# A memory loop in feature-major form with a Gram-matrix correction, in a four-block network on one core

## Chip, cores and metric

One core of one Trainium2 chip. The metric is the device time in microseconds of one execution. The time of a kernel is the median over its runs.

## What is computed

A batch of 4 images, 16 x 16 positions, 64 channels, all float32, goes through four blocks, each added to its input: a test-time memory (below), a mixture of eight experts of which two are used, a stack of convolutions, and an LSTM over the 256 positions. Only the first block is touched. With its names:

```python
mem0 = ((w1_0, w2_0), (w1_1, w2_1))            # 64x128 and 128x64, twice
def _mlp(params, h):
    for w1, w2 in params:
        h = h + gelu(h @ w1) @ w2
    return h
def step(carry, x_t):                          # x_t: 4 images, 16 tokens, 64 channels
    params, mom = carry
    k = _l2norm(x_t @ Wk); v = x_t @ Wv
    lr, forget, eta = ...                      # one number per image, a mean of sigmoids
    g = grad of mean((_mlp(params, k) - v)**2)
    new_mom = eta * mom - lr * g
    new_params = params * (1 - forget) + new_mom
(paramsT, momT), _ = scan(step, (params0, mom0), swapaxes(x, 0, 1))   # 16 steps
final = mean of paramsT over the images
return _mlp(final, q)
```

Each image has its own weights. The sixteen steps depend on each other: the weights after one step are those of the next.

## The kernel before

The kernel is written with an instruction list for each engine and explicit semaphores; nothing reorders them. Stages in order: the inputs' layer norm, projections, gates (lines 322 to 354 on TensorE); the memory loop; the final pass of all 1024 tokens through the averaged weights (466 to 490); the experts; the convolutions; the LSTM (654 to 675), an unrolled loop of 256 steps in which TensorE does six small products with 64x64 weights (L651) and three or four fills (L675).

**Weights.** P holds the weights, M the momentum, each 128 partitions x 4 images x 256 columns. Columns 0:128 hold w1_0 on partitions 0:64 and w1_1 on partitions 64:128; columns 128:192 hold w2_0 and 192:256 w2_1, both over 128 partitions. Me and Pf are M and P times their gate, Q is their sum. GpSimd computes these three each step (L282, L283, L286), on whole tiles of 1024 elements a partition. The layout is the same for the four images.

**The loop.** `Fori(0, T, MEM_UN)` on every engine, four steps in the body, so four passes. GpSimd copies the step's keys, values and gates into small tiles (kcur, vcur, gcur, lrcur) one step ahead. A step works token-major in the hidden layers: tokens of image b lie on partitions 32b to 32b+15. Forward: a0 (L366, TensorE), gelu on ScalarE (L727), a transpose back to feature-major (L373) and a copy, h1 (L380), a1 (L393), gelu (L742), again a transpose and a copy, the prediction (L407). VectorE adds keys and values (L930, L933, L943) and computes the gelu's derivative from a square and a tanh of ScalarE (L927, L928, L935, L937 for the first layer, L939 to L949 for the second). Backward: L416, L438, L449 with transposes of the weights made in the same step (L375, L386, L402), and of the errors; then sixteen gradient products (L428, L456, L461, L462) into four PSUM banks, one for each image. When all are there (semaphore grads), VectorE adds them in three instructions: both halves of P (L960, L961) and M (L962). The next step's a0 waits for the first of them.

**Fills.** `keep_busy(place, bank)` (L316) issues matmuls of zeros, 256 bf16 columns each, whose result nobody reads, ahead of a wait of TensorE. BUSY gives their number at twelve places of a step: 38 in all, ten at the start, four behind a0. `busy` (L312) does the same with 512 columns outside the loop; eight such stand behind the loop and begin when P's second half is done.

**After the loop.** VectorE adds the four images' weights (L966, L967), scales them (L968), and L471 is the first product of the final pass.

Of the kernel before, what the change touches and what calls it, by code (L numbers as in the profile page):

```python
# [20 lines left out]
DE = 128  # L21
# [4 lines left out]
S = W * W  # L26
# [11 lines left out]
BUSY = (10, 4, 4, 2, 2, 0, 5, 5, 4, 0, 4, 2)  # L38
MEM_UN = 4
TP = T + MEM_UN  # L40


def wide(ap, n):

    return bass.AP(ap.tensor, ap.offset, [*ap.ap, [0, n]])
# [7 lines left out]
def build(nc, i_, out):  # L53
    with ExitStack() as ctx:
# [18 lines left out]
        memw = sb("memw", [128, 2 * DE])  # L73
# [43 lines left out]
        kk = sb("kk", [128, B, TP * C])  # L117
        qq = sb("qq", [128, NTOK])
        vT = sb("vT", [128, B, TP * C])
        kcur = [sb(f"kcur{n}", [128, B, 32]) for n in range(2)]  # L120
        vcur = [sb(f"vcur{n}", [128, B, C]) for n in range(2)]
        gcur = [sb(f"gcur{n}", [128, 3, B]) for n in range(2)]
        lrcur = [sb(f"lrcur{n}", [128, 1]) for n in range(2)]
# [12 lines left out]
        w21T = sb("w21T", [128, B, DE])  # L136
        w20T = sb("w20T", [128, B, DE])
        w11T = sb("w11T", [128, B, D])
        g0T = sb("g0T", [128, B, C])
        g1T = sb("g1T", [128, B, C])  # L140
        h1T = sb("h1T", [128, B, 32])
        dT = sb("dT", [128, B, 32])
        dh1T = sb("dh1T", [128, B, 32])
        da1T = sb("da1T", [128, B, C])
        hv = sb("hv", [128, B, C])
        a0q, a0u, a0y, a0t, a0x, a0s = (sb(f"a0{c}", [128, DE]) for c in "quytxs")
        a1q, a1u, a1y, a1t, a1x, a1s = (sb(f"a1{c}", [128, DE]) for c in "quytxs")
        g0tok = sb("g0tok", [128, DE])
        h1tok = sb("h1tok", [128, D])
        g1tok = sb("g1tok", [128, DE])  # L150
        dtok = sb("dtok", [128, D])
# [3 lines left out]
        ktok = sb("ktok", [128, D])  # L155
        FW2 = sb("FW2", [128, 2, 2 * DE])
        FW = sb("FW", [128, 2 * DE])
# [22 lines left out]
        hT = sb("hT", [128, E, HC, NTOK // 2])  # L180
        yT = [sb(f"yT{n}", [128, NTOK // 2]) for n in range(2)]
        fold = sb("fold", [128, D])
# [39 lines left out]
        def _(sp):  # L222
            sp.dma_start(xs[:, :, :], i_["x"]).then_inc(sem("ld_x"), 16)
            for dst, key, s in ((ident[:, :], "ident", "ld_id"), (wqkv[:, :], "wqkv", "ld_a"), (wgate[:, :], "wgate", "ld_a"),
                                (gaff[:, :], "gaff", "ld_g"), (gsel[:, :, :], "gsel", "ld_g"), (memw[:, :], "memw", "ld_m"),
# [15 lines left out]
        def _(pool):  # L241
            nc.gpsimd.memset(idle[:, :], 0.0)
            nc.gpsimd.memset(xnT[:, :], 0.0).then_inc(sem("idle"), 1)  # L243
            for t in (*kcur, h1T, dT, dh1T):
                nc.gpsimd.memset(t[:, :, :], 0.0)
            nc.gpsimd.memset(M[:, :, :], 0.0)
# [21 lines left out]
            def kview(tile, t, lo=0):  # L268
                return tile[lo:128, :, bass.ds(t * C, C)]
# [918 lines left out]
```

## Time and profile before

| | us |
|---|---|
| runs | 800.73, 807.91, 808.19 |
| median | 807.91 |
| the profiled execution's own time | 796.82 |
| its span, first to last instruction | 795.0 |
| the sixteen memory steps | 31.2 to 353.6 |

The page gives busy times, shares of the span, and the granted clock of TensorE in tenths of 2.4 GHz. In the chain of waits each piece is the time that one group adds to the chain, from its start to the next piece's; in the views of lines and of the timeline the time is that of the instructions themselves, which overlap on TensorE. A float32 matmul has two records, a transpose or a bf16 matmul has one. Durations below come from the one profiled execution.

### The profile page before, as it was taken

To read this page: it belongs to the slowest core of one execution; us is meant where nothing else is said; L and a number is where in the kernel's file an instruction comes from. 1 tells how busy PE (TensorE), PEld (TensorE's weight loads), DVE (VectorE), ACT (ScalarE), POOL (GpSimd) and SP (SyncE) were. 2 spreads that over 40 slices of the span, in tenths; PEclk is the share of its full clock that TensorE was granted. 3 is DMA by queue.
4 is the path that set the end of the run, shared out by engine and by line. 5 is a ranking of instruction groups with operands and counts; after the bars stand their busy time and mean duration, and the time that the engine had idled before them with its cause. 6 is when DMAs were issued, how large, how long until landed. Compare 5 with 4: busy or idle time off the path is not lost.

```text
span 795.0 us, 17274 instructions
## 1 busy us (share of the span) xinstructions
PE 744.4 (94%) x6999; PEld 429.6 (54%) x7007; DVE 353.2 (44%) x1243; ACT 236.1 (30%) x1138; POOL 122.7 (15%) x148
## 2 busy tenths in 40 slices
PE   7788899999999999979898999999999999999997
PEld 3555555556655565545323855555555555555554
DVE  2654444444344434464656044444444444444443
ACT  2422222222222222213651013333333333333332
POOL 3333333333333323330000000000000000000000
PEclk9986666655566556667999999999999999999999
DMA  7000000000000000000000000000000000000000
GB/s 257 22 1 2 2 0 0 0 0 0 0 0 0 0 0 0 0 0 1 1 0 1 0 1 2 2 2 2 2 2 2 2 2 2 3 2 2 2 2 14
DMA packets 2995, 6.62 MB, mean 8 GB/s; under 512 B 1650, under 2 KB 2295, under 8 KB 2807
## 3 DMA queue, kind: packets, MB, share of 16 engines
q1 hardware_dynamic: 2934, 5.79, 2.1%
q8 instruction: 41, 0.67, 0.4%
q14 instruction: 20, 0.16, 0.1%
HBM read 5.52 MB, written 0.26 MB: 7 GB/s over the span
## 4 chain that ended last, share of the span: by engine, by line
PE 85%; DVE 10%; issue 2%; POOL 1%; ACT 1%; another core or an unknown queue 0%; DVEq 0%; POOLq 0%; ACTq 0%
PE bk L675 26%; PE bk L316 14%; PE bk L651 11%; PE bk L428 4%; DVE a0y L935 3%; PE bk L607 3%; PE bk L312 2%; PE bk L645 2%; PE bk L535 2%; PE bk L438 2%; DVE hv L933 2%; PE bk L553 2%; PE bk L380 1%; PE bk L456 1%; PE bk L461 1%
## 5 line engine op out<-in xcount | busy, mean ns | idle before, releaser
L675 PE MATMUL bk<-idle 128*64 128x512 bf16 (+1 forms) x930 | 226.2, 362 | 0.0
L316 PE MATMUL bk<-idle 128*128 128x256 bf16 x608 | 139.7, 381 | 2.7 <-POOL lrcur L266 2.7
L651 PEld LDWEIGHTS bk<-mem,lvh 64*64 64x64 f32 x3072 | 79.6, 132 | 86.0 <-DVE mem L1103 86.0
L675 PEld LDWEIGHTS bk<-idle 128*64 128x64 bf16 x930 | 81.4, 109 | 51.0
L651 PE MATMUL bk<-mem,lvh 64*64 64x4 f32 x3072 | 102.2, 203 | 0.4 <-DVE mem L1103 0.4
L1100 DVE TENSOR_TENSOR_SCAN bk<-gx 128x16 f32<-128x16 f32 x256 | 51.1, 200 | 114.5 <-ACT gx L832 114.5
L832 ACT ACTIVATE gx<-bk 128x8 f32<-128x8 f32 x256 | 47.1, 184 | 157.4 <-PE bk L651 157.4
L316 PEld LDWEIGHTS bk<-idle 128*128 128x128 bf16 x608 | 65.2, 126 | 40.5 <-issue 11.2
L1103 DVE SCALAR_TENSOR_TENSOR mem<-og,bk 128x4 f32<-128x4 f32 x256 | 40.7, 159 | 57.4 <-ACT bk L836 57.4
L282 POOL TENSOR_TENSOR mem<-mem,gcur 128x1024 f32<-128x1024 f32 x16 | 30.3, 1893 | 202.4 <-DVE mem L962 202.1
L836 ACT ACTIVATE bk<-bk 128x4 f32<-128x4 f32 x256 | 40.4, 158 | 49.9 <-DVE bk L1100 49.9
L1106 DVE SCALAR_TENSOR_TENSOR gx<-mem,bk 128x4 f32<-128x4 f32 x255 | 41.2, 162 | 8.9
L834 ACT ACTIVATE og<-bk 128x4 f32<-128x4 f32 x256 | 44.5, 174 | 0.0
L286 POOL TENSOR_TENSOR mem<-mem 128x1024 f32<-128x1024 f32 x16 | 37.5, 2346 | 1.3
L935 DVE SCALAR_TENSOR_TENSOR a0y<-a0s,a0y 128x128 f32<-128x128 f32 x16 | 36.6, 2288 | 0.5
L312 PE MATMUL bk<-idle 128*128 128x512 bf16 x100 | 28.6, 443 | 5.1 <-POOL xnT L243 2.3
L428 PE MATMUL bk<-dtok,g1tok 16*128 16x64 f32 x128 | 32.3, 435 | 0.0
L727 ACT ACTIVATE g0tok<-bk 128x128 f32<-128x128 f32 x16 | 4.4, 277 | 91.0 <-PE bk L366 91.0
L283 POOL TENSOR_TENSOR mem<-mem,gcur 128x1024 f32<-128x1024 f32 x16 | 30.3, 1894 | 0.0
L416 PE MATMUL bk<-w21T,dT 64*16 64x128 f32 x128 | 8.8, 356 | 21.8 <-DVE dT L943 21.8
L960 DVE TENSOR_TENSOR mem<-mem,bk 128x512 f32<-128x512 f32 x16 | 11.0, 687 | 40.9 <-PE bk L462 40.9
L428 PEld LDWEIGHTS bk<-dtok,g1tok 16*128 16x128 f32 x128 | 23.4, 300 | 10.4 <-issue 9.7
(275 smaller groups left out, 835.4 us busy)
## 6 DMA issues: line engine op xcount, KB each, us to landing
cw<-in_cw SPq DMA_DIRECT2D x1, 3456.0 KB, 11.0
w<-in_w SPq DMA_DIRECT2D x2, 512.0 KB, 3.5
xs<-in_x SPq DMA_DIRECT2D x1, 256.0 KB, 2.7
out<-xs SPq DMA_DIRECT2D x1, 256.0 KB, 3.2
memw<-in_memw SPq DMA_DIRECT2D x1, 128.0 KB, 2.1
lu<-in_lu SPq DMA_DIRECT2D x1, 97.5 KB
wqkv<-in_wqkv SPq DMA_DIRECT2D x1, 96.0 KB, 2.5
lv<-in_lv SPq DMA_DIRECT2D x1, 96.0 KB
```

The costliest lines, as they stand in the source:

```text
L312: nc.tensor.matmul(bk[:, bank, 0:512], idle[:, 0:128], idle[:, 128:128 + 512], start=True, stop=True)
L316: nc.tensor.matmul(bk[:, bank, 0:256], idle[:, 0:128], idle[:, 128:128 + 256], start=True, stop=True)
L428: nc.tensor.matmul(bk[:, 4 + b, 192:256], g1tok[r, :], dtok[r, :], start=True, stop=True)
L651: return nc.tensor.matmul(bk[HALF[n], 3 * (s // CH % 2) + g, c:c + B], lvh[HALF[k], g, :], hist[HALF[k], s, :], start=False, stop=True, sk ...
L675: nc.tensor.matmul(bk[0:D, 7, 0:n], idle[:, 0:D], idle[:, 128:128 + n], start=True, stop=True)
L832: nc.scalar.activation(gx[:, :, :, 2], bk[:, bank:bank + 2, cols], ACT.Tanh).then_inc(sem("in_gate"), 1)
L834: nc.scalar.activation(og[:, :], bk[:, bank + 2, cols], ACT.Tanh)
L836: nc.scalar.activation(tanh_c, cs[:, s % 2, :, 3], ACT.Tanh, scale=0.5).then_inc(sem("tanh_c"), 1)
L935: nc.vector.scalar_tensor_tensor(a0y[:, :], a0s[:, :], -1.0, a0y[:, :], ALU.add, ALU.mult).then_inc(sem("a0z"), 1)
L1100: nc.vector.tensor_tensor_scan(c_t.rearrange(flat4), gx[:, 1, :, :].rearrange(flat4), gx[:, 0, :, :].rearrange(flat4), 0.0, ALU.add, ALU.m ...
L1103: nc.vector.scalar_tensor_tensor(hist[:, s + 1, :], og[:, :], 1.0, tanh_c, ALU.add, ALU.mult).then_inc(sem("h_new"), 1)
L1106: nc.vector.scalar_tensor_tensor(gx[:, 1, :, 3], hist[:, s + 1, :], 0.5, c_t[:, :, 3], ALU.mult, ALU.mult).then_inc(sem("hc"), 1)
```

## The change

The memory loop is written anew; the stages behind it stay, but for where the final weights come from.

- The hidden layers are feature-major: a0, a1 and their gradients have the 128 features on the partitions and 4 x 16 tokens along the free dimension, so ScalarE and VectorE work on 64 elements a partition instead of 128, and the activations need no transpose on the forward way. What the gradients need in token form is transposed in one group of four later (toks), and dz and da1T by one transpose each.
- Images 2 and 3 have the two layers' halves swapped (KIND, KROW, HROW, COL20, COL21), and matmuls go in the order 0, 2, 1, 3 (PAIRS). The input memw comes in both layouts.
- The next step's a0 is no longer taken from the updated weights. It is built from the old ones: P with decayed keys kf, plus M with kf's counterpart ke, both computed once ahead of the loop, plus the gradient's part, which is the key Gram matrix of the two steps (gram, computed ahead for all steps, scaled by the learning rate) times da0tok. These are 8 + 8 + 4 matmuls of 64x64 weights.
- The update is split. P's second half is added when the gradients are there; M's first half by four instructions with the gate as a scalar; P's first half in the next step, behind h1z; M's second half in the next step too, behind gap_mid. GpSimd decays half tiles: Pf of each half, Me of the second, Q of the second.
- y and z of the gelu's derivative lie in PSUM.
- Fills: GAP = (2, 4, 1, 1), eight a step instead of 38.
- The loop is unrolled over 16 steps on every engine, with no registers and no prefetch copies.
- Ahead of the loop: transposes of all keys, 60 Gram products, their scaling, the masks swap, dup and fold, and the decayed keys on GpSimd. Behind it: FS, FZ, a matmul with dup, FW1 and FW2 in place of FW; the eight `busy` matmuls follow that matmul.

The diff, cut to its core:

```diff
-BUSY = (10, 4, 4, 2, 2, 0, 5, 5, 4, 0, 4, 2)
-MEM_UN = 4
+GAP = (2, 4, 1, 1)
+LO, HI = slice(0, D), slice(D, 2 * D)
+KIND = (0, 0, 1, 1)
+PAIRS = (0, 2, 1, 3)
...
+            def gap(place, bank):
+                for _ in range(GAP[place]):
+                    ins = nc.tensor.matmul(bk[:, bank, 256:512], idle[:, 0:128], idle[:, 128:128 + 256], start=True, stop=True)
+                return ins
...
+            for t in range(T):
+                pool.wait_ge(sem("p2_new"), t + 1)
+                decay(Pf, P, 1, C2, t).then_inc(sem("decay2"), 1)
+                pool.wait_ge(sem("p1_new"), t + 1)
+                decay(Pf, P, 1, C1, t).then_inc(sem("pf1"), 1)
+                pool.wait_ge(sem("m2_new"), t + 1)
+                decay(Me, M, 0, C2, t).then_inc(sem("decay2"), 1)
+                pool.wait_ge(sem("decay2"), 2 * t + 2)
+                nc.gpsimd.tensor_tensor(Q[:, :, C2], Pf[:, :, C2], Me[:, :, C2], ALU.add).then_inc(sem("Q2"), 1)
...
+            def a0_products(w, k, first):
+                for b in PAIRS:
+                    c = (b % 2) * C
+                    for e in (LO, HI):
+                        ins = nc.tensor.matmul(bk[e, KIND[b], c:c + C], w[KROW[b], b, e], k[KROW[b], b, 0:C],
+                                               start=first and b % 2 == 0, stop=True, skip_group_check=True)
+                return ins
...
+            for t in range(T):
+                n = t + 1
+                pe.wait_ge(sem("g0T"), n)
+                pe.wait_ge(sem("p2_new"), n)
+                for b in PAIRS:
+                    ins = nc.tensor.matmul(bk[HROW[b], 2, b * C:(b + 1) * C], P[:, b, COL20[b]], g0T[:, b, 0:C], start=True, stop=True)
+                ins.then_inc(sem("h1_ps"), 1)
+                for b in range(B):
+                    ins = nc.tensor.transpose(bk[:, 3, b * DE:(b + 1) * DE], P[:, b, DE:2 * DE], ident[:, :])
+                ins.then_inc(sem("w2T_ps"), 1)
+                if t:
+                    pe.wait_ge(sem("m1_new"), B * t)
+                    gap(1, 7).then_inc(sem("gap_mid"), 1)
+                pe.wait_ge(sem("p1_new"), n)
+                pe.wait_ge(sem("y0"), n)
+                pe.wait_ge(sem("h1z"), n)
...
+                ins.then_inc(sem("a1T"), 1)
+                pe.wait_ge(sem("w2T"), n)
...
+                ins.then_inc(sem("w1T_ps"), 1)
+                pe.wait_ge(sem("hv"), n)
+                pe.wait_ge(sem("g1T"), n)
...
+                ins.then_inc(sem("pred_ps"), 1)
+                pe.wait_ge(sem("w1T"), n)
+                pe.wait_ge(sem("r0T"), n)
+                for k, tile in enumerate((g0T, h1z, r0T, g1T)):
+                    ins = nc.tensor.transpose(bk[:, 3, k * DE:(k + 1) * DE], tile[:, :, :].rearrange("p b c -> p (b c)"), ident[:, :])
+                ins.then_inc(sem("toks_ps"), 1)
+                pe.wait_ge(sem("y1"), n)
+                pe.wait_ge(sem("dz"), n)
...
+                ins.then_inc(sem("dg1_ps"), 1)
+                nc.tensor.matmul(bk[:, 2, 64:64 + B * C], swap[:, :], dz[:, :, 0:C], start=True, stop=False, skip_group_check=True)
+                pe.wait_ge(sem("toks"), n)
+                nc.tensor.transpose(bk[:, 3, 0:DE], dz[:, :, :].rearrange("p b c -> p (b c)"), ident[:, :]).then_inc(sem("dtok_ps"), 1)
+                gap(2, 7)
+                pe.wait_ge(sem("da1T"), n)
...
+                ins.then_inc(sem("dh1_ps"), 1)
+                pe.wait_ge(sem("dtok"), n)
...
+                nc.tensor.transpose(bk[:, 3, 256:384], da1T[:, :, :].rearrange("p b c -> p (b c)"), ident[:, :]).then_inc(sem("d1tok_ps"), 1)
+                gap(3, 7)
+                pe.wait_ge(sem("dh1z"), n)
...
+                ins.then_inc(sem("dg0_ps"), 1)
...
+                if n < T:
+                    pe.wait_ge(sem("k_decayed"), 2)
+                    a0_products(P, kf[:, n, :, :], True)
+                    a0_products(M, ke[:, n, :, :], False)
+                pe.wait_ge(sem("d1tok"), n)
...
+                pe.wait_ge(sem("da0tok"), n)
...
+                ins.then_inc(sem("grads"), 1)
+                if n < T:
+                    for k, rows in enumerate((LO, HI)):
+                        for e in (LO, HI):
+                            ins = nc.tensor.matmul(bk[e, k, 0:32], da0tok[rows, e], gram[rows, t, 32 * k:32 * k + 32], start=False,
+                                                   stop=True, skip_group_check=True)
+                    ins.then_inc(sem("a0T"), 1)
+                    gap(0, 3)
...
+            for t in range(T):
+                dve.wait_ge(sem("q0"), n)
...
+                nc.vector.tensor_tensor(h1z[:, :, 0:C], h1_ps, kz[:, t, :, :], ALU.add).then_inc(sem("h1z"), 1)
+                if t:
+                    dve.wait_ge(sem("pf1"), t)
+                    dve.wait_ge(sem("m1_new"), B * t)
+                    nc.vector.tensor_tensor(P[:, :, C1], Pf[:, :, C1], M[:, :, C1], ALU.add).then_inc(sem("p1_new"), 1)
+                nc.vector.tensor_tensor(hv[:, :, :], h1_ps, kv[:, t, :, :], ALU.add).then_inc(sem("hv"), 1)
+                if t:
+                    dve.wait_ge(sem("gap_mid"), t)
+                    nc.vector.tensor_tensor(M[:, :, C2], Me[:, :, C2], bk[:, 4:8, C2], ALU.add).then_inc(sem("m2_new"), 1)
...
+                dve.wait_ge(sem("grads"), n)
+                dve.wait_ge(sem("Q2"), n)
+                nc.vector.tensor_tensor(P[:, :, C2], Q[:, :, C2], bk[:, 4:8, C2], ALU.add).then_inc(sem("p2_new"), 1)
+                for b in range(B):
+                    nc.vector.scalar_tensor_tensor(M[:, b, C1], M[:, b, C1], gates[:, 0, b, t:t + 1], bk[:, 4 + b, C1], ALU.mult,
+                                                   ALU.add).then_inc(sem("m1_new"), 1)
```

## Rows read from the trace of the kernel before

**Rows 1.** The page: busy time, granted clock in 40 slices, chain by engine.
```profile
PE 744.4 (94%) x6999; PEld 429.6 (54%) x7007; DVE 353.2 (44%) x1243; ACT 236.1 (30%) x1138; POOL 122.7 (15%) x148
...
PEclk9986666655566556667999999999999999999999
...
PE 85%; DVE 10%; issue 2%; POOL 1%; ACT 1%; another core or an unknown queue 0%; DVEq 0%; POOLq 0%; ACTq 0%
```

**Rows 2.** Stretches: length, busy time (instructions) by engine, clock, DMA share, GB/s.
```profile
31.19:44.27 13.08, 13.08 (x146) 8.80 (x146) 6.03 (x17) 5.26 (x18) 4.37 (x6) 0.97 0.01 2
...
146.81:166.97 20.16, 18.41 (x146) 11.25 (x146) 9.24 (x17) 5.26 (x19) 6.93 (x8) 0.67 0.00 0
166.97:188.73 21.76, 21.76 (x146) 13.20 (x146) 8.47 (x17) 5.26 (x19) 6.84 (x8) 0.50 0.00 0
...
31.19:353.40 322.21, 298.99 (x2302) 183.08 (x2302) 145.27 (x269) 84.12 (x288) 110.67 (x114) 0.64 0.00 0
```

**Rows 3.** The chain through a half-clock step: start us, us, piece.
```profile
167.19 0.97 PE bk L316 x4
...
169.00 0.96 PE bk L380 x8
169.96 0.99 PE bk L386 x4
...
171.38 0.56 PE bk L393 x8
171.93 0.30 PE bk L396
...
178.63 0.41 PE bk L432
...
184.02 0.64 PE bk L456 x8
184.66 0.54 PE bk L316 x2
185.20 0.40 PE bk L461
...
185.86 2.25 PE bk L316 x10
```

**Rows 4.** Groups by line, 146.0 to 166.2 us: busy us, mean ns | idle before.
```profile
L935 DVE SCALAR_TENSOR_TENSOR a0y<-a0s,a0y 128x128 f32<-128x128 f32 x1 | 2.5, 2457 | 0.0
...
L286 POOL TENSOR_TENSOR mem<-mem 128x1024 f32<-128x1024 f32 x1 | 2.3, 2343 | 0.1
...
L960 DVE TENSOR_TENSOR mem<-mem,bk 128x512 f32<-128x512 f32 x1 | 0.7, 686 | 2.6 <-PE bk L462 2.6
...
L416 PE MATMUL bk<-w21T,dT 64*16 64x128 f32 x8 | 0.4, 273 | 1.8 <-DVE dT L943 1.8
```

**Rows 5.** Line 935 in all sixteen steps, durations in ns, min/median/max.
```profile
L935 DVE SCALAR_TENSOR_TENSOR a0y<-a0s,a0y x16: 292/2458/2465, 34.8 to 338.5; 128x128 f32<-128x128 f32 x16
```

**Rows 6.** The chain through a mixed step (146.8 to 167.0 us).
```profile
148.56 0.58 PE bk L380 x8
...
155.07 1.18 PE bk L316 x5
```

**Rows 7.** The chain through one step of the LSTM.
```profile
600.32 0.34 PE bk L651 x12
```

**Rows 8.** The chain through step 1 of the loop, at full clock.
```profile
32.73 0.57 PE bk L380 x8
...
39.93 0.54 PE bk L316 x4
...
42.67 1.20 PE bk L316 x10
```

**Rows 9.** The chain behind the loop, from the last gradients on.
```profile
353.56 0.03 issue
...
358.58 2.29 PE bk L471 x4
```

More of the change, by code:

```diff
@@ L135, in build @@
         Q = part(4 * WB, B, 2 * DE)
[L136 to L151, printed above, removed]
+        w2T = sb("w2T", [128, B, DE])
+        w1T = sb("w1T", [128, B, DE])
+        g0T, r0T, g1T, da1T, h1z, dz, dh1z = (sb(n, [128, B, 32]) for n in ("g0T", "r0T", "g1T", "da1T", "h1z", "dz", "dh1z"))
+        toks = sb("toks", [128, 4, DE])
+        g0tok, h1tok, r0tok, g1tok = (toks[:, n, :] for n in range(4))
+        dtok = sb("dtok", [128, DE])
         da1tok = sb("da1tok", [128, DE])
@@ L243, in _ @@
             nc.gpsimd.memset(xnT[:, :], 0.0).then_inc(sem("idle"), 1)
-            for t in (*kcur, h1T, dT, dh1T):
+            for t in (g0T, r0T, g1T, da1T, h1z, dz, dh1z):
                 nc.gpsimd.memset(t[:, :, :], 0.0)
+            nc.gpsimd.memset(kk[:, :, :, C:], 0.0)
+            for t in (kz, kv):
+                nc.gpsimd.memset(t[:, :, :, :], 0.0)
             nc.gpsimd.memset(M[:, :, :], 0.0)
-            nc.gpsimd.memset(gates[:, :, :, :], 0.0)
-            nc.gpsimd.memset(lrtok[:, :], 0.0)
-            nc.gpsimd.memset(kk[:, :, S:], 0.0)
-            nc.gpsimd.memset(vT[:, :, S:], 0.0)
             nc.gpsimd.memset(sc0[:, :, :], 0.0)
@@ L470, in _ @@
+            pe.wait_ge(sem("FZ"), 1)
+            nc.tensor.matmul(bk[:, 0, 0:2 * DE], dup[:, :], FZ[:, :], start=True, stop=True).then_inc(sem("FW1_ps"), 1)
+            busy(AFTER[0], 1)
+            pe.wait_ge(sem("FW1"), 1)
             for n in range(2):
[L471 removed]
+                nc.tensor.matmul(bk[:, 2 + n, :], FW1[:, 0:DE], qq[:, n * 512:(n + 1) * 512], start=True,
                                  stop=True).then_inc(sem("f_a0"), 1)
+            pe.wait_ge(sem("FW2"), 1)
@@ new lines, in _ @@
+            dve.wait_ge(sem("ld_id"), 16)
+            nc.vector.tensor_copy(swap[:, 0:D], ident[:, D:2 * D])
+            nc.vector.tensor_copy(swap[:, D:2 * D], ident[:, 0:D])
+            for k in range(2):
+                nc.vector.tensor_tensor(dup[:, k * D:(k + 1) * D], ident[:, 0:D], ident[:, D:2 * D], ALU.add)
+            nc.vector.tensor_tensor(fold[:, :], ident[:, 0:D], ident[:, D:2 * D], ALU.add).then_inc(sem("masks"), 1)
+            dve.wait_ge(sem("lrtok"), 4)
+            dve.wait_ge(sem("ktok_ps"), 1)
@@ new lines, in _ @@
+            dve.wait_ge(sem("pf1"), T)
+            dve.wait_ge(sem("m1_new"), B * T)
+            nc.vector.tensor_tensor(P[:, :, C1], Pf[:, :, C1], M[:, :, C1], ALU.add).then_inc(sem("p1_new"), 1)
+            dve.wait_ge(sem("p2_new"), T + 1)
+            nc.vector.tensor_tensor(FS[:, 0, :], P[:, 0, C2], P[:, 1, C2], ALU.add)
+            link(nc.vector.tensor_tensor(FS[:, 1, :], P[:, 2, C2], P[:, 3, C2], ALU.add))
+            dve.wait_ge(sem("p1_new"), T + 1)
+            for k in range(2):
+                nc.vector.tensor_tensor(FZ[KROW[2 * k], C1], P[KROW[2 * k], 2 * k, C1], P[KROW[2 * k], 2 * k + 1, C1], ALU.add)
+                ins = nc.vector.tensor_tensor(FZ[HROW[2 * k], C2], P[HROW[2 * k], 2 * k, C1], P[HROW[2 * k], 2 * k + 1, C1], ALU.add)
```

484 lines of the change are left out of this document (218 added, 266 removed).

## The prediction

> **What bounds the kernel now.** I read the page first: TensorE is the engine with work nearly all the time, and it carries 85% of the chain that ended last; its clock is low just in the slices of the memory loop [rows 1]. Then the busy times by stretch: the sixteen steps take 322.2 of 795.0 us at a mean clock of 0.64. Step 1 at nearly full clock (2.4 GHz) took 13.08 us, steps at half clock (1.2 GHz) 21.76 us, with TensorE busy through the whole step, and mixed ones some 20.2 us [rows 2]. So at half clock a step is bound by what TensorE has in its queue, by nothing else. Then the chain of waits through a half-clock step: every piece is TensorE, and its fills (L316, 38 matmuls in nine pieces, the first 0.97 and the last 2.25) are 9.03 of the 21.76 us; the other groups are 12.73 us [rows 3]. Last the other engines: VectorE spends 2.5 us at L935, which took 0.29 us once, while GpSimd runs its three products and sums (L286 the longest). At half clock TensorE's queue covers that; at full clock it is the reason for a 1.8 us hole in TensorE ahead of L416, and the clock then falls: L380 took 0.58 early in that step (full clock), five fills 1.18 behind the hole (half) [rows 4 to 6].
>
> **The part replaced, at half clock.** All 38 fills go (9.03 us) and eight come: two, four, one and one. Four cost 0.97, two 0.54 and one about 0.21, so 0.97 + 0.54 + 0.42 = 1.93 us. The other TensorE work of a new step, group by group, with the nearest row of the half-clock step [rows 3]:
> - h1, prediction and dh1: three groups of four matmuls, 128x64 weights and 16 columns, as L380: 3 x 0.96 = 2.88. Their outputs now alternate between column halves, which may let two run side by side; the nearest row with split columns, L393, is 0.56, so 1.7 is the lower end.
> - Three groups of four transposes (second layers, first layers, token forms), as L386: 3 x 0.99 = 2.97; single transposes of dz and da1T, 0.30 each as L396: 0.60; the swap matmul, as L432: 0.41.
> - a1 and dg1: eight matmuls each with 64x64 weights. Before shows that form only in the LSTM, twelve records in 0.34 us at full clock [rows 7]. Sixteen are 0.45, and by L380's ratio of the two clocks (0.96 to 0.57) [rows 3, 8] 0.76 at half: 1.52 together. Bounds 0.9 to 2.0.
> - Next step's a0 before the new weights exist: sixteen such matmuls, 1.5 (0.9 to 2.0), and the Gram correction, four of them with 32 columns, 0.38.
> - dh1 and dz in token form: sixteen records with 16-column weights; L393's eight with twice the columns are 0.56, I take 0.8. dg0: 0.55, as L393.
> - The gradients: as L456 0.64 twice, and the last two groups together as L461/L462, from 185.20 to 185.86, 0.66: 1.94.
>
> That makes 2.88 + 2.97 + 0.60 + 0.41 + 1.52 + 1.50 + 0.38 + 0.80 + 0.55 + 1.94 = 13.55, with fills 15.5 us. So the rewriting removes no TensorE work other than fills: 12.73 becomes about 13.5, with 176 matmul records against 146 [rows 2]. By the lower ends of the groups it is 13.1 with fills, by the upper ones 16.5. I take 15.0, between the row-by-row sum and the overlap of the column halves, and add 0.3 us for a wait (below): **15.3 us for a half-clock step**.
>
> **What hides what.** From the gradients' semaphore of step t: VectorE adds P's second half (0.69, row L960), then four M updates, some 0.2 apart (0.85), then u0, y0, h1z at 2.3 us, then P's first half (0.69) at 3.0 (durations by L960 and by L935 undisturbed) [rows 4, 5]. TensorE meanwhile has the Gram group, two fills, h1, four transposes, four fills: 0.38 + 0.54 + 0.96 + 0.99 + 0.97 = 3.8 us. So a1, which waits for P's first half, finds it done 0.8 us earlier. P's first half stands in VectorE's queue ahead of hv and, behind gap_mid, M's second half (0.69), z0 and r0T: these end at about 4.8 us, u1 and y1 at 5.2; ScalarE's tanh, square and w1T copy (0.3 + 0.3 + 0.6) end near 6.3, when TensorE, after pred, is at about 6.0. That is the 0.3 us wait. Later waits (tokens 0.6 us behind dg1, dh1z 0.2 behind the token group, dtok, d1tok) each have a TensorE group in front of them that is longer. GpSimd has three products and one sum, each over half of what L286 covers in 2.3 us, so at most 4 x 1.2 = 4.8 us [rows 4], spread over 15; p2_new waits for nothing there. Moving a0's first product ahead of the update takes the end of the old chain away (grads, P, M, ten fills, L366, gelu): the a0 of the next step is out 0.4 us after the gradients.
>
> At full clock the same groups by the rows of step 1 (L380 0.57, four fills 0.54) sum to 9.1 us [rows 8], but a1 now waits for P's first half (3.05 us), and the token transposes wait for w1T: 2.2 us of waits, so **11.3 us at full clock**. The two SBUF-input operations whose collision cost 2.5 us are gone: y and z now lie in PSUM.
>
> One such operation is left, P's first half. L935 took 292 ns once and 2458 ns in the median, the second case beside a GpSimd instruction [rows 5]; if P's first half met one, it would be held by up to 1.2 us, and 0.8 us of that is covered at half clock. In my order GpSimd's first product ends at about 1.9 us and its next waits for P's first half itself, so I price it at nothing. The Trainium skill, "SBUF — State Buffer", section "Who interferes with whom", says that a VectorE instruction with two SBUF inputs and a GpSimd instruction that reads SBUF exclude each other; by it too the meeting depends on the order alone.
>
> **Prologue and tail.** Before, step 0's gradients ended at 42.7, where the ten fills start [rows 8]. New on VectorE ahead of the loop: a PSUM clear of 1024 elements (at most 1.4, twice L960), swap, dup and fold (five times 0.2), four scalings of 512 elements (2.8, as L960) [rows 4]; the copies of vT and qq make room for subtractions of much the same length. TensorE has 16 transposes and 60 small Gram matmuls, some 2 + 4 us, which end near 33.5; the last two scalings wait for them. So the loop's VectorE starts at 35, and step 0's gradients end near 47 at half clock (44 at full): +4.3 us. At the end, from the gradients (353.56) to L471 (358.58) it was 5.0 us [rows 9]. Now P, M x4, P, FS, FZ in a row take 3.8, then the dup matmul, and the eight fills now follow it (8 x 0.43, less what overlaps): 7.5, +2.5 us.
>
> **The sum.** The fifteen steps from one gradients' end to the next took 353.56 - 42.67 = 310.9 us (20.7 each) [rows 8, 9]. At half clock throughout they take 15 x 15.3 = 229.5: -81.4. With +4.3 and +2.5: -74.6. I take off 4 us more for one step or two at full clock, since step 1 had it before [rows 2]. The rest (experts, convolution, LSTM) is untouched. The profiled execution took 796.8 us (span 795.0 and 1.8 around it), the runs shown 800.7, 807.9 and 808.2, so the median is 11.1 above it and the lowest 3.9. 796.8 - 78.6 = 718; I put 8 us on top, as some of that excess is likely the clock's changing share in the loop that is now shorter: **726 us**.
>
> **Why mostly half clock.** In the old loop full clock came back for (0.67 - 0.5) / 0.5 of 20.16, or 6.9 us, of a mixed step, after the ten and four fills that stand nearly in a row there, and it was lost at the 1.8 us hole; the step behind had none of it, though TensorE's queue was never empty [rows 2, 6]. The new loop has eight fills, no row of ten, and small matmuls in their place. I see nothing that brings the clock back more often.
>
> **Rivals.**
> - *Full clock for most of the loop.* The 2.5 us collision, after which the clock fell, is gone, and a full-clock step has no hole over 0.9 us. For it: step 1 before kept full clock and took 13.08 us [rows 2]. Against: the fills' share falls from 41% to 13% of a half-clock step. 15 x 11.3 = 169.5: -141.4 + 1.5 + 1 = -139, so 658 and, with the 8, 666 us. Chance 0.17.
> - *Changes of form cost more than my groups.* The new step has about eighteen changes of weight shape, and two fills behind L456 took 0.54 where two at 0.21 are 0.43: 0.1 each, partly in my rows. At 0.12 more for each, 17.5 us a step: -48.4 + 6.8 = -41.6, 763 us. Chance 0.16. The Trainium skill, "TensorEngine Tiling (Array Packing)", section "Key Properties", says that a change of tiling mode drains the engine. It gives no price; by it this rival is the one to expect, by the rows the drain is mostly inside the groups.
> - *Slower than before: a half-clock step costs by record, not by column.* 21.76 us over 146 records is 149 ns for each with its load; 176 would be 26.2 us, 15 x 26.2 = 393: +82 + 7, so 886 and, with the 8, 894 us. It decides from 20.3 us a step, 115 ns a record. Against it: L461/L462 put sixteen records in 0.66 us, the LSTM twelve in 0.34 [rows 3, 7]. Chance 0.03.
> - *It gains next to nothing*, because a wait I have as covered (p1_new through GpSimd's pf1, or toks) ends each step at about 20 us, so -10.9 + 6.8 = -4, and 801 us: 0.02.
>
> **How the numbers follow.** My case, 13.7 to 16.6 us a half-clock step, is 726 - 24 = 702 to 726 + 20 = 746 us, chance 0.62. A range to leave out no more than 0.2 takes in part of both neighbours: 664 to 767. About 1% is what a measurement of this kernel can tell from no change. Faster by over 1%: 0.95; within 1% (the last rival): 0.02; slower 0.03.
>
> **What would show it.** Steps (one gelu of g0T to the next) of 15 to 16 us at clock 0.50 to 0.6; TensorE busy over 90% of the step; the eight fills at 1.9 us a step; no VectorE operation of the loop over 1 us; h1z some 2.3 us behind the gradients; loop from 35 to about 276 us. Steps of 11 us at clock 0.9 would prove me wrong on the clock; TensorE idle for over 2 us a step, on a wait I called covered; TensorE busy but over 17 us, on the groups' prices.

## The result, and the profile after

| | us |
|---|---|
| after: median of 4 runs (lowest, highest) | 699.67 (692.21, 701.53) |
| before, same chip: median of 4 runs (lowest, highest) | 804.32 (792.06, 808.19) |
| ratio, 95% interval | 0.8768 [0.863, 0.8906] |
| the profiled execution, its span | 701.53, 699.5 |

The kernel is faster by 12.3%. 699.7 us lies inside the range of 664 to 767 and 26 us under the 726 forecast. It is also 2 us below the 702 to 746 of my own case: only the part of the range that was added for a neighbouring case holds it. The page of the new kernel first, the lines that answer to [rows 1]:

```profile
span 699.5 us, 18288 instructions
...
PE 661.7 (95%) x7611; PEld 397.3 (57%) x7611; DVE 301.7 (43%) x1325; ACT 221.5 (32%) x1076; POOL 90.0 (13%) x101
...
PEclk7755555555555557899999999999999999999998
```

TensorE still has work nearly all the time, and the digits of its clock say at what speed: 5 (half clock, 1.2 GHz) through the memory loop, 9 behind it. Next the steps themselves. The first view gives all instructions of the line of the first gelu (times in ns, then the first and last start), the second the busy time of each engine in the whole loop and in one step:

```profile
L747 ACT ACTIVATE g0T<-bk x16: 224/224/224, 35.4 to 243.1; 128x64 f32<-128x64 f32 x16
```

```profile
core 0: us, PE busy (x) PEld busy (x) DVE busy (x) ACT busy (x) POOL busy (x), PEclk, DMA share, GB/s
35.40:243.10 207.70, 201.21 (x2635) 141.00 (x2636) 83.77 (x320) 64.49 (x210) 64.96 (x59) 0.50 0.01 2
119.80:133.50 13.70, 13.46 (x178) 9.43 (x176) 5.47 (x22) 4.27 (x16) 4.41 (x4) 0.50 0.00 1
```

The first step takes 15.57 us (from one gelu to the next), and each of the fourteen behind it 13.73 us, at a clock of 0.50, with TensorE busy for 13.46 of 13.70 us. Before, steps were 13.1 to 21.8 us at a mean clock of 0.64 [rows 2]. So the loop got shorter although, in this execution, it lost the part of the time at full clock that it had.

The chain of waits through one such step (start, what the piece adds, both us; pieces that say nothing more are left out):

```profile
130.62 0.98 PE bk L360 x32
...
132.90 0.37 PE bk L474 x8
133.26 0.54 PE bk L311 x2
...
133.84 0.62 PE bk L386 x8
134.46 1.05 PE bk L389 x4
135.50 0.87 PE bk L311 x4
...
138.19 0.48 ACT w1T L763
...
138.71 1.12 PE bk L416 x4
139.83 0.56 PE bk L424 x16
140.38 0.62 PE bk L426 x2
...
141.43 0.55 PE bk L433 x8
141.97 0.34 PE bk L439 x8
```

The chain leaves TensorE once, from 136.4 to 138.7, for the way over M's second half (which waits for the four fills), z0, r0T, u1, the tanh, the square and w1T. TensorE wasn't idle there: a1, the first layers' transposes and the prediction ran beside it, and it waited for w1T for 0.2 us at the end. The eight fills are 0.54 + 0.87 + 0.21 + 0.21 = 1.83 us, against 9.03 before [rows 3]. Of VectorE's operations in the loop the one with two SBUF inputs is P's first half (fifteen of them from 49 us on):

```profile
L984 DVE TENSOR_TENSOR mem<-mem 128x512 f32<-128x512 f32 x15 | 10.2, 682 | 0.0
```

All take 0.68 us, and no GpSimd instruction ran beside any of them: in the step shown GpSimd's first product ended at 134.82 us, P's first half took from 135.04 to 135.72, and the next product began at 135.80. Before, L935 took 2.46 us in the median [rows 5].

### The profile page after: what moved, and what is told of

It is laid out like the page before. It is cut to its first block, busy times and chain, and to the rows that moved or that the text cites. A ratio compares the mean times of both kernels' runs of the same rounds, so it can differ in the third digit from the quotient of the medians.

```text
span 699.5 us, 18288 instructions
## 1 busy us (share of the span) xinstructions
PE 661.7 (95%) x7611; PEld 397.3 (57%) x7611; DVE 301.7 (43%) x1325; ACT 221.5 (32%) x1076; POOL 90.0 (13%) x101
## 4 chain that ended last, share of the span: by engine, by line
PE 86%; DVE 7%; ACT 3%; issue 2%; POOL 1%; DVEq 0%; ACTq 0%; POOLq 0%
PE bk L690 30%; PE bk L666 12%; PE bk L311 4%; PE bk L622 3%; PE bk L307 3%; PE bk L416 3%; PE bk L660 2%; PE bk L550 2%; PE bk L389 2%; PE bk L360 2%; PE bk L568 2%; PE bk L452 1%; PE bk L460 1%; PE bk L426 1%; PE bk L463 1%
## 5 line engine op out<-in xcount | busy, mean ns | idle before, releaser
L273 POOL TENSOR_TENSOR mem<-mem,gates 128x512 f32<-128x512 f32 x48 | 50.2, 1047 | 143.3 <-DVE mem L1013 120.9
L311 PE MATMUL bk<-idle 128*128 128x256 bf16 x122 | 38.5, 418 | 0.0
L1114 DVE TENSOR_TENSOR hT<-hT,bk 128x1024 f32<-128x1024 f32 x16 | 19.5, 1221 | 13.4 <-ACT hT L802 6.9
L802 ACT ACTIVATE hT<-bk,b1e 128x512 f32<-128x512 f32 x32 | 20.0, 685 | 13.3 <-PE bk L550 13.2
L747 ACT ACTIVATE g0T<-bk 128x64 f32<-128x64 f32 x16 | 3.6, 224 | 60.0 <-PE bk L474 52.6
L307 PEld LDWEIGHTS bk<-idle 128*128 128x128 bf16 x105 | 11.3, 112 | 18.7 <-issue 8.2
L284 POOL TENSOR_TENSOR mem<-mem 128x512 f32<-128x512 f32 x16 | 20.2, 1266 | 1.3
L660 PE MATMUL bk<-mem,lu 65*128 65x64 f32 x96 | 20.4, 297 | 0.0
L550 PE MATMUL bk<-x2A,w1g 64*128 64x512 f32 x64 | 19.8, 689 | 0.0
L311 PEld LDWEIGHTS bk<-idle 128*128 128x128 bf16 x122 | 16.8, 149 | 3.8
```

Of the source, the lines that this page charges most:

```text
L273: return nc.gpsimd.tensor_tensor(dst[:, :, cols], src[:, :, cols], wide(gates[:, g, :, t], DE), ALU.mult)
L307: nc.tensor.matmul(bk[:, bank, 0:512], idle[:, 0:128], idle[:, 128:128 + 512], start=True, stop=True)
L311: ins = nc.tensor.matmul(bk[:, bank, 256:512], idle[:, 0:128], idle[:, 128:128 + 256], start=True, stop=True)
L660: nc.tensor.matmul(bk[:, 3 * (chunk % 2) + g, 0:CH * B], lu[:, g, :], t3T[:, chunk * CH:(chunk + 1) * CH, :], start=True, stop=False, skip ...
```

## The experiments

Twelve kernels ran, each beside the kernel before on the same chip; ratios are to that, in brackets their 95% intervals. The step is read from one g0T gelu to the next. The kernel with the other order of images below does the same work and its runs lie closer together: 0.8793 [0.8736, 0.8849]. It is a second reference where the new kernel's own interval is too wide. Where intervals still overlap, the step or the stretch in the trace decides.

**Fewer fills in the kernel before.** Nine fills a step, each at the place of one that was there:

```diff
-BUSY = (10, 4, 4, 2, 2, 0, 5, 5, 4, 0, 4, 2)
+BUSY = (1, 1, 1, 1, 1, 0, 1, 1, 1, 0, 1, 1)
```

> The kernel before with one fill at each of the nine places that have any, 9 a step instead of 38; nothing else is changed, so it has about as many fills as the new kernel (8). My theory: most of what the change gained is the fills that it left out. TensorE's part of a half-clock step falls from 21.76 by 29 x 0.213 = 6.2 to 15.6 us, and the VectorE and GpSimd collisions are about covered; the time falls by some 15 x 5.4 = 81 us, to a ratio of 0.90. Rival: the rewriting itself is what gained, because without fills the old step waits for VectorE held behind GpSimd (L933, L935); then the step stays over 18 us and the ratio is 0.95 or more.

Measured: 757.16 us, ratio 0.9514 [0.9451, 0.9578], most steps 17.8 us at half clock. My own expectation, a ratio near 0.90, failed; the rival's 0.95 came, with a step just under the 18 us that it named. The chain of one step says why, and below it two instructions of the same step in order of time:

```profile
138.40 1.90 DVE a0y L935
...
140.32 1.83 DVE a0x L937
```

```profile
140.22 2.35 POOL L286 TENSOR_TENSOR mem<-mem 128x1024 f32<-128x1024 f32 x1
...
140.32 2.39 DVE L937 SCALAR_TENSOR_TENSOR a0x<-a0y,a0t 128x128 f32<-128x128 f32 x1
```

Once the fills no longer cover it, TensorE waits for VectorE: L935 and L937 put 3.73 us on the chain, where their shortest instances take 0.29 us [rows 5] and 0.38. L937 lasts as long as GpSimd's sum L286 beside it; L935 takes 1.89 us beside the product L283 (1.90). In the old loop it was mostly one of the two that was held: L935 at 2.46 us and L937 at 0.38 in the median, 2.84 together against 4.28 in the step here. So the fills of the old loop hid the collision with GpSimd, and without them it also grew; taking 29 of 38 fills away gives 38 us (795.0 to 757.2). The new kernel lies another 57 us below that, 4.0 us a step: so much comes with the rewriting.

**y and z back in SBUF.** The new kernel, with y0, z0, y1 and z1 in an SBUF tile:

```diff
-            y0, z0, y1, z1 = (bk[:, 4, 256 + 64 * n:256 + 64 * (n + 1)].rearrange("p (b c) -> p b c", b=B) for n in range(4))
+            y0, z0, y1, z1 = (yz[:, n, :, :] for n in range(4))
```

> y0, z0, y1 and z1 go to SBUF instead of PSUM; nothing else changes. In the kernel before, the operations with both inputs in SBUF took up to 2.5 us beside a GpSimd product. Theory (the choice of PSUM for y and z is a part of the gain): r0T, z0, z1 or x1 meet a GpSimd product in each step and are held by 0.5 to 1.3 us; z0 and r0T have slack behind w1T's chain, so 0.3 to 1.5 us a step come through, +5 to +22 us, 705 to 722 us. Rival: in the new order no such operation stands beside a GpSimd product (three products near 1.05 us and a sum of 1.27 us in 13.7 us), so the same operations keep their 0.13 to 0.25 us and the time stays within 2 us of 699.7.

Measured: 709.9 us, ratio 0.8927 [0.8887, 0.8966], the step 14.53 us, +0.80 (but two steps of 13.46, whose mean clock was 0.63). All the instances of r0T's line first in the new kernel, then in this one, and then two instructions of this one in order of time:

```profile
L992 DVE SCALAR_TENSOR_TENSOR r0T<-bk,t x16: 224/225/225, 40.6 to 247.1; 128x64 f32<-128x64 f32 x16
```

```profile
L993 DVE SCALAR_TENSOR_TENSOR r0T<-yz,t x16: 1036/1037/1285, 39.8 to 255.9; 128x64 f32<-128x64 f32 x16
```

```profile
140.58 1.05 POOL L274 TENSOR_TENSOR mem<-mem,gates 128x512 f32<-128x512 f32 x1 [0.31 <-DVE mem L989]
...
140.67 1.04 DVE L993 SCALAR_TENSOR_TENSOR r0T<-yz,t 128x64 f32<-128x64 f32 x1
```

r0T starts 0.09 us behind GpSimd's product and ends 0.08 us behind its end at 141.63: it waited for the whole product, each time, because VectorE's M update both releases that product and stands right ahead of z0. u1 is queued behind it, and w1T behind u1. The theory holds: the home of y and z in PSUM is worth 0.80 us a half-clock step. The Trainium skill, "SBUF — State Buffer", section "Who interferes with whom", says that a VectorE instruction with two SBUF inputs contends with a GpSimd instruction that reads SBUF. This pair of rows agrees: 1.04 us with two, 0.23 us with one.

**All outputs of two groups in one column half.**

```diff
-                    ins = nc.tensor.matmul(bk[HROW[b], 2, b * C:(b + 1) * C], P[:, b, COL20[b]], g0T[:, b, 0:C], start=True, stop=True)
+                    ins = nc.tensor.matmul(bk[LO, 2, b * C:(b + 1) * C], P[:, b, COL20[b]], g0T[:, b, 0:C], start=True, stop=True)
```

and the same in the prediction (L411). This kernel puts h1 and the prediction of images 2 and 3 in rows where they don't belong, so its values are wrong; it is here for its times alone.

> The four matmul pairs of h1 and of the prediction all write output partitions 0 to 63, where the new kernel writes images 2 and 3 to partitions 64 to 127; so h1 and the prediction of two images land in the wrong rows, and the memory's values are not the reference's. Dh1 and everything else stay. Theory (outputs in two column halves let two matmuls run side by side, and that is what made these groups cheaper than L380 of the kernel before): the h1 group and the prediction group take 0.96 us again instead of 0.62, dh1 keeps 0.55; the step is 13.73 + 2 x 0.34 = 14.4 us, the whole +10 us, some 709 us. Rival (the records of this program are denser for another reason, such as weights that lie in another place or the neighbouring groups): the two groups stay at 0.6 to 0.7, the step at 13.7 to 13.9 and the time at 699 to 702 us.

```profile
137.02 1.00 PE bk L386 x8
138.03 1.05 PE bk L389 x4
139.07 0.85 PE bk L311 x4
139.93 0.56 PE bk L401 x16
140.48 1.04 PE bk L405 x4
141.53 0.97 PE bk L411 x8
```

The two groups take 1.00 and 0.97 us, as L380 before (0.96) [rows 3], instead of 0.62: the column halves are the cause. The Trainium skill, "TensorEngine Tiling (Array Packing)", section "Key Properties", says that different tiles work in parallel, and the rows agree. Twelve steps take 14.25 us, 0.52 more than 13.73, since the longer groups also swallow the wait of 0.2 us for w1T. But the time stayed at 698.5 us, ratio 0.8752 [0.8709, 0.8795]: in the profiled execution two steps had full clock for part of their time (a mean clock of 0.77) and took 11.07 us each. Twelve times +0.52 and twice -2.66 leave +0.9, and the loop is 1.2 us longer (208.9 for 207.7). The price of the groups is shown, the expected +10 us didn't come.

**The order of the images.** `PAIRS = (0, 1, 2, 3)` for `(0, 2, 1, 3)`, so that two images of one column half follow each other:

> The new kernel with PAIRS = (0, 1, 2, 3): the same matmuls, but two in a row now go to the same half of the columns (or of the rows). If the alternation is why a group of four (L386) takes 0.62 us where the old L380 took 0.96: three groups 0.34 longer each, the 64x64 groups up to 0.2 each, so a step of 14.8 to 15.6 us and 16 to 28 us more. If it comes from something else, within 4 us of the new kernel.

Measured: 699.01 us, ratio 0.8793 [0.8736, 0.8849], the group of L386 at 0.62 us as with the other order, the steps 13.77 us and one, at a mean clock of 0.78, 10.72. That the alternation is what lets the halves overlap fell; that there are two halves is enough for four matmul pairs.

**Without the Gram correction.** In each step VectorE writes M and P's first half before anything else, and a0 is one product with the new weights:

```diff
-                if n < T:
-                    pe.wait_ge(sem("k_decayed"), 2)
-                    a0_products(P, kf[:, n, :, :], True)
-                    a0_products(M, ke[:, n, :, :], False)
...
+                    pe.wait_ge(sem("p1_new"), n + 1)
+                    a0_products(P, kk[:, n, :, :], True).then_inc(sem("a0T"), 1)
```

> The Gram correction is left out: in the loop, a0 of the next step is computed from the updated weights, as in the kernel before, in the new feature-major form. VectorE writes M and P of the first layers first; TensorE waits for P's first half, then eight matmuls instead of twenty-four with the Gram group. Theory A (TensorE's queue sets the step): 0.98 + 0.37 us of matmuls go and 0.5 come, and TensorE waits for M x4 and P's first half, 1.1 + 0.7 us less what the fills cover (0.54), and then for u0, q0, g0T; the step is 14.4 to 15.2 us instead of 13.73, +10 to +22 us in all, 710 to 722 us. Theory B (the Gram correction costs as much as it saves): the step stays at 13.5 to 14.0 us and the time at 696 to 703 us.

```profile
132.81 1.14 DVE mem L1002 x4
...
134.04 0.70 DVE mem L1006
...
134.78 0.67 PE bk L360 x16
...
135.47 0.23 ACT g0T L740
```

Measured: 707.9 us, ratio 0.8906 [0.8866, 0.8945], the step 14.65 us (but two steps of 13.29 and 12.23, at mean clocks of 0.63 and 0.78). The four pieces above, 2.74 us, now stand in a row between the gradients and h1, where the new kernel has 0.91 us (the Gram group and two fills) and, ahead of the gradients, a0's 0.98. Theory A holds: the Gram-matrix part is worth 0.9 us a step against this order of VectorE's work. The first of the four pieces, M's updates at 1.14 us, is there only because P's first half is made from M here. With P's first half as one addition, as in the last kernel below, the step without the Gram part would be about 14.65 - 1.14 = 13.5 us (an estimate, not run). So the 0.9 us holds for this order of updates, and may be nothing in another.

**The number of fills in the new kernel.** `GAP = (2, 4, 1, 1)` is eight. Run with one, `(0, 1, 0, 0)`, twenty, `(5, 7, 4, 4)`, and 38, `(10, 12, 8, 8)`:

> The new kernel with GAP = (0, 1, 0, 0), one fill a step instead of eight. My theory: the loop is at half clock with or without them, and each fill costs its 0.213 us where TensorE is what the others wait for: the four of gap_mid also delay M's second half on VectorE. Step 13.73 - 0.64 - 0.4 = 12.7 us, 15 us less in all (ratio to the new kernel about 0.98). Rival: the fills stand in waits and cost nothing, so the time stays within 3 us.

> The new kernel with GAP = (10, 12, 8, 8), the 38 fills a step of the kernel before. If activity brings full clock back for part of the loop: clock 0.6 to 0.9, step 15 to 18 us, 20 to 65 us more than the new kernel. If the loop stays at half clock: step 13.73 + 30 x 0.213 = 20.1 us, 96 us more.

> Twenty fills in a step (five, seven, four and four) where the new kernel has eight; nothing else. Theory A (the small matmuls of the new loop don't hold the clock, and twenty fills are too few to bring it back): all steps at half clock, 13.73 + 12 x 0.21 = 16.3 us, the whole 699.7 + 15 x 2.5 = 738 us. Theory B (the clock comes back part of the time, as with 38 fills, where steps took 12.5 to 15.3 us): a mix of full-clock steps near 11.3 us and half-clock ones near 16.3 us, the whole 690 to 725 us.

| fills | us | ratio | steps, us | mean clock of the loop |
|---|---|---|---|---|
| 1 | 684.57 | 0.8607 [0.8551, 0.8663] | 12.75 | 0.50 |
| 8 | 699.67 | 0.8768 [0.863, 0.8906] | 13.73 | 0.50 |
| 20 | 690.46 | 0.8645 [0.8572, 0.8718] | 11.6 to 15.5 | 0.74 |
| 38 | 703.03 | 0.8824 [0.8758, 0.889] | 12.5 to 15.3 | 0.87 |

The granted clock in slices, with 20 fills and then with 38 (the loop is slices 3 to 14):

```profile
PEclk9755866769988878999999999999999999999999
```

```profile
PEclk9769879989899977899999999999999999999999
```

The time doesn't follow the number of fills in one direction. The intervals of eight and twenty overlap; the second reference (0.8736 at its lower end) is just above twenty's 0.8718, and the loops of the profiled executions, first gelu to last, are 207.7 and 198.7 us. With twenty, theory B holds: full clock comes back for part of the loop, its fastest steps take 11.6 to 12.2 us and its slowest 15.5, and the sum is below that with eight. With 38 my expectation failed: I had 20 to 65 us more than the new kernel and steps of 15 to 18 us, and it was 3.4 us more. The clock is full for most of the loop, and the fills themselves use up the gain. With one, all is at half clock, and the step is shorter by 0.98 us where seven fills were 1.6: the rest has become a wait, since TensorE now waits for VectorE, whose updates stand on the chain from the gradients to u1 (as in the kernel with one fill shown below).

**The prologue.** GpSimd's products kf and ke wait until VectorE has written the masks:

```diff
+            pool.wait_ge(sem("masks"), 1)
             for dst, g in ((kf, 1), (ke, 0)):
```

> GpSimd starts its two products of the decayed keys (kf, ke) only when VectorE has written the masks, so that they don't stand beside the four copies of the rates. Theory: these four copies (SBUF to SBUF, 32 partitions x 16) took 4.93 us in the new kernel because GpSimd's two products ran beside them, and 0.76 us in the kernel before; then they take under 1 us, the loop's first VectorE operation starts near 35.5 instead of 39.5 us, step 0's first gelu 3 to 4 us earlier, and the whole takes some 696 (3 to 4 us less than the new kernel's 699.7). GpSimd ends kf and ke near 42 instead of 36.3 us, and the a0 products of step 1, near 50, still find them. Rival: something else sets the loop's start (the Gram matmuls, which end near 33.3, and the scalings behind them); then the start moves by under 1 us and the time stays at 699 to 700.

The instructions grouped by line, VectorE's copies and GpSimd's products in the new kernel, then the copies in this one (count, busy us, mean ns of one):

```profile
L941 DVE COPY lrtok<-gates 32x16 f32<-32x16 f32 x4 | 4.8, 1210 | 0.1
```

```profile
L268 POOL TENSOR_TENSOR hT<-kk,gates 128x960 f32<-128x960 f32 x2 | 3.8, 1908 | 1.3 <-DVE gates L937 1.3
```

```profile
L942 DVE COPY lrtok<-gates 32x16 f32<-32x16 f32 x4 | 0.7, 167 | 0.1
```

Measured: 694.21 us, ratio 0.8721 [0.8685, 0.8758]; the loop's first g1T gelu starts at 35.0 instead of 40.8 us, more than the 3 to 4 us expected. The ratio's interval overlaps the new kernel's; the earlier start is what shows the gain. Copies of 16 elements, one SBUF input each, took 1.2 us in the mean beside GpSimd and 0.17 us without it.

**The tail.** The eight wide fills behind the loop go ahead of the wait for FZ:

```diff
+            busy(AFTER[0], 1)
             pe.wait_ge(sem("FZ"), 1)
             nc.tensor.matmul(bk[:, 0, 0:2 * DE], dup[:, :], FZ[:, :], start=True, stop=True).then_inc(sem("FW1_ps"), 1)
-            busy(AFTER[0], 1)
```

> The eight fills behind the loop are issued ahead of the dup matmul that waits for FZ, as in the kernel before they stood in VectorE's last updates. Theory: the 3.41 us of these fills are on the path from the last gradients to the final product L485; they go beside VectorE's 4.2 us of updates, and the final product comes 8.8 - 2.8 = about 6 us behind the gradients, the whole takes about 697 us. Rival: TensorE's clock, not the wait, sets that stretch: the fills are needed there to bring the clock back, and with an idle hole behind them the two final matmuls and the 16 that follow run at half clock, so that under 1 us is gained.

The chain of the new kernel, then that of this one, and then each kernel's stretch from its last gradients to the end of L516 (length, busy times, clock):

```profile
259.45 1.22 PE bk L481 x2
260.67 3.41 PE bk L307 x8
264.09 2.54 PE bk L485 x4
```

```profile
259.01 0.71 PE bk L482 x2
...
260.18 1.98 PE bk L485 x4
```

```profile
255.33:276.92 21.59, 17.45 (x93) 10.64 (x94) 9.15 (x38) 4.47 (x8) 1.85 (x2) 0.74 0.00 1
```

```profile
254.89:272.46 17.57, 16.17 (x93) 9.59 (x92) 9.15 (x38) 4.47 (x8) 1.85 (x2) 0.89 0.00 1
```

The stretch is 4.0 us shorter, more than the 2.8 expected: its clock is 0.89 instead of 0.74, since the same fills run while TensorE would have stood idle, and the two products behind them are shorter. The rival, that the fills are missed there, fell. The whole took 697.1 us, ratio 0.8748 [0.8708, 0.8788]; that interval by itself overlaps the new kernel's, so it is the stretch that shows the gain.

**Together, and one step on.** One fill, the prologue's wait and the tail's order in one kernel:

> One fill instead of eight in a step, kf and ke after the masks, and the eight fills behind the loop ahead of FZ, all three together. If the effects add up (one fill alone 684.6, the prologue -5.5, the tail -2.6 us), 676 to 679 us; the step as with one fill, 12.75 us. Rival: the tail's gain was part of the noise of its runs and the step with one fill is now bound by VectorE, so that an earlier start is all that is kept: 679 to 681 us.

Measured: 678.27 us, ratio 0.8505 [0.8467, 0.8543]: the effects add up to within 2 us (684.6 - 5.5 - 2.6 = 676.5), and the step is 12.75 us as with one fill. VectorE's part of its step:

```profile
133.98 0.69 DVE mem L1015
134.66 1.03 DVE mem L1017 x4
...
136.09 0.60 DVE mem L986
```

These, and M's second half (0.66 at 136.76), stand in a row between the gradients and u1. The last kernel takes M out of it: GpSimd makes Q for the first half too, and P's first half is one addition behind P's second; M's halves are written later, and no fill is left in the loop:

```diff
+                decay(Me, M, 0, C1, t).then_inc(sem("me1"), 1)
...
+                nc.gpsimd.tensor_tensor(Q[:, :, C1], Pf[:, :, C1], Me[:, :, C1], ALU.add).then_inc(sem("Q1"), 1)
...
-                for b in range(B):
-                    nc.vector.scalar_tensor_tensor(M[:, b, C1], M[:, b, C1], gates[:, 0, b, t:t + 1], bk[:, 4 + b, C1], ALU.mult,
-                                                   ALU.add).then_inc(sem("m1_new"), 1)
+                nc.vector.tensor_tensor(P[:, :, C1], Q[:, :, C1], bk[:, 4:8, C1], ALU.add).then_inc(sem("p1_new"), 1)
```

> Built on the kernel with one fill and the two moves (678.3 us, 12.75 us a step, with VectorE's updates on the path from the gradients to a1). No fills in the loop; GpSimd also decays M's first half and adds Pf and Me for it, so that P's first half is one VectorE operation directly behind P's second half (0.7 us), M's first half one of 0.7 us instead of four of 0.26, and M's second half comes behind y1. Theory: a1 waits for TensorE's own groups (0.7 + 0.62 + 1.05 us behind the gradients) instead of for P's first half at 2.75 us, u1 comes at about 3.5 instead of 3.9 us, and the step takes 12.2 to 12.5 us; behind the loop 1.7 us of updates go. 678.3 - 15 x 0.4 - 1.5 = 671 us (669 to 675). Rival: the step was bound by the chain from g1T to w1T and by TensorE behind it, and GpSimd's five products and sums a step (6.7 us) now meet one of VectorE's or come late: the step stays at 12.75 or grows, 677 us or more.

```profile
132.90 0.70 DVE mem L1016
...
133.74 0.62 PE bk L393 x8
134.35 1.06 PE bk L396 x4
...
135.44 0.60 ACT w2T L758
```

Measured: 672.34 us, ratio 0.8417 [0.8365, 0.8468], the fastest version here. The whole is as the theory said, its step is not quite: 12.57 us where 12.2 to 12.5 was expected. P's first half is gone from the chain; in its place the chain now goes over ScalarE's copies of the transposed weights (w2T 0.60 us, and w1T 0.59), which TensorE waits for.

## Why the prediction was right, and which terms were off

**The bound and the clock: right.** In the profiled execution every step behind the first is at half clock and TensorE has work for 98% of it, as said. Full clock for most of the loop (chance 0.17) didn't happen. Single steps with part of their time at full clock turned up in four of the other kernels with eight fills (those of the order, the one column half, y and z in SBUF, and no Gram correction). They also show that my 11.3 us for a step at full clock was too long: the one of 10.72 us had full clock for little more than half of its time (mean 0.78). The 4 us taken off for a step or two at full clock didn't come in the profiled execution.

**The step: 13.73 us for the 15.3 forecast, at the very edge of the case's 13.7 to 16.6.** Term by term from the chain above (a1 and the first layers' transposes from the run with one column half, where they are on the chain):
- h1, prediction and dh1: 2.88 forecast at the form of L380, 0.62 + 0.62 + 0.55 = 1.79 measured (the prediction's 0.62 is the length of its instructions, as it isn't on the chain). This is the term that was mis-sized most: the lower end, "two run side by side", was the right one, and I left it as a bound. The run with one column half showed it.
- The 64x64 products: a0 1.50 forecast, 0.98 measured; a1 and dg1 1.52, measured 0.56 + 0.56. The LSTM's rows [rows 7] scaled by the clock ratio overprice them; a1's sixteen records take 0.56 us at half clock.
- dh1 and dz in token form: 0.80 forecast, 0.34 + 0.21 measured.
- The other way: the three groups of transposes 2.97 forecast, 1.05 + 1.04 + 1.12 measured, and the swap matmul 0.41 forecast, 0.62 measured.
- Fills 1.93 against 1.83, Gram 0.38 against 0.37, dg0 (L448 in the chain) 0.55 against 0.56: as forecast. The gradients were 1.94 as forecast. Taken together the terms give 13.6 us, and the wait for w1T is 0.2 us, not 0.3: 13.8 for the 13.73 measured.

**The rivals.** Changes of form at 0.12 us each would have made the step 17.5 us; the sums above leave no room for it. The Trainium skill's rule of a drain ("TensorEngine Tiling (Array Packing)", "Key Properties") is not refuted by that, but here its price is at most what the groups already hold: h1 with its two changes of form took 0.62 us. Cost by record fell likewise: 178 matmul records in 13.70 us are 77 ns each, against 149 at half clock before. The covered waits stayed covered: p1_new, toks and da1T put nothing on the chain with eight fills.

**The collision: right in the order, too cheap as a gain.** I priced P's first half at nothing, and all its instances took 0.68 us. What I didn't weigh is how much of the gain depends on it. I said that the rewriting removes no TensorE work other than fills and treated the collision as covered at half clock. Covered it was, but by the fills that were to go: with nine of them left it costs the old form some 3 us a step (3.73 less the undisturbed 0.29 and 0.38). That this didn't spoil the total is because I priced the new step for itself and not the old one less the fills.

**Prologue: the term that failed for a reason.** "The loop's VectorE starts at 35" was 39.5 (step 0's gradients at 50.5, not 47), because my sum has no term for the four rate copies, which leaves them at their old 0.8 us, and I didn't ask what GpSimd does at that moment; the new kf and ke products stand right there. **Tail:** 8.8 us from the last gradients to the final product against 7.5: the updates with FS and FZ took 4.1 us for 3.8, the fills 3.41 as priced, and the dup matmul 1.22 us, for which the sum leaves about 0.3.

**The sum.** Gradients of step 0 to those of step 15: 255.3 - 50.5 = 204.8 us against 225.5 forecast, -20.7; prologue +3.5, tail +1.3: 718 - 15.9 = 702 us, and the profiled execution took 701.5. The 8 us on top were wrong too: the median, 699.7, lies 1.9 us below the profiled execution and not above it, as that was the slowest of the four. Their spread is 9.3 us, and the fastest, 692.2 us, has the highest mean clock, 0.829 against 0.814 in the profiled one. So the clock's share still changes from run to run. Some three steps like the one of 10.72 us would account for the difference (an estimate: 3.0 us each); no trace of that run shows it.

The 26 us between the forecast and the median are thus the loop's 20.7 and the 8 and 1.9 us of the spread, less the 4.8 of prologue and tail. The mechanism was right, but the terms of the loop were priced high by 1.6 us a step, and it was the width of the range that covered it.

Two things stay open. What decides whether a step with eight fills gets some full clock isn't shown: one or two steps of fifteen did in four kernels, none in the profiled executions of the new kernel and of those with the prologue and the tail changed. And the 4.0 us a step that came with the rewriting are shown only in part: y and z in PSUM (0.80), the Gram part (0.92) and the column halves of two groups (0.52) were each taken back alone, 2.2 us in all. How much of the 4.0 is the collision that went away is not known, since GpSimd's work in the old form was not changed alone.

## What to carry to other kernels

Before fills are taken out, ask what else they cover: here nine fills instead of 38 gave 38 us, and the other 57 came with the rewriting, in which the held operations on VectorE are gone too. Small products whose outputs lie in both column halves should be priced lower than those in one: here 0.62 us against 1.00 for the same eight records. And when an engine gets new work in the prologue, look which short instructions of another engine stand beside it, and put fills where the engine is idle anyway, ahead of the wait and not behind it.

## What was unexpected of the hardware

- Four copies of 32x16 elements from SBUF to SBUF took 0.16, 1.86, 1.83 and 0.98 us, the second and third as long as GpSimd's products of 1.9 us beside them, and 0.17 us each without them. I had thought of the collision only for operations with two SBUF inputs.
- Fills at four places of a step and the time: 684.6 us with one, 699.7 with eight, 690.5 with twenty, 703.0 with 38. The clock grows (0.50, 0.50, 0.74, 0.87 in the loop) and so do the fills' costs: of these four numbers one fill is the best, and eight is worse than twenty by the loops' 207.7 and 198.7 us.
- Eight wide fills moved ahead of a wait took 4.0 us off the tail, 0.5 of them in the dup matmul and 0.6 in L485 (1.22 to 0.71 and 2.54 to 1.98 us), in a stretch whose clock went from 0.74 to 0.89.
